# A routed expert stage on one core: blank rows in front of each expert's region instead of behind its last row, and last tiles that overlap

## The reference

```
x = x + ln(attn(ln(x)))                      # state-space block
logits = xf @ Wr + br; probs = softmax(logits)
vals, idx = top_k(probs, 2); w = vals / vals.sum(-1)
for ei in range(16):
    h = silu(xf @ W1[ei]) * (xf @ W3[ei])    # 128 -> 512
    y = layernorm(h @ W2[ei]) * gamma[ei] + beta[ei]
    out = out + combine[:, ei:ei + 1] * y
x = x + ln(out)
```

## Time and profile before

| What | Value |
|---|---|
| Median of 3 runs | 968.94 us (967.91 to 969.12) |
| Profiled execution | 968.34 us, of which the span of instructions is 966.5 us |
| Mean granted TensorE clock | 0.99 |
| PE busy | 933.1 us (97%) |
| DVE, ACT, POOL busy | 724.8, 688.3, 621.8 us |
| POOL stores of stage 2 (L698) | 143, 148.2 us busy |
| DMA share of the 16 engines | q1 18.4%, q0 5.2% |

### The profile page before, as it was taken

How to read it: one execution, slowest core, us unless ns; L and a number is a source line. 1 busy time by engine, 2 the same in 40 slices (tenths; PEclk the granted TensorE clock), 3 DMA queues, 4 the chain that set the end, 5 groups by cost and what they waited for, 6 DMA issues and landing times.

```text
span 966.5 us, 26600 instructions
## 1 busy us (share of the span) xinstructions
PE 933.1 (97%) x7177; PEld 826.0 (85%) x7177; DVE 724.8 (75%) x2524; ACT 688.3 (71%) x1355; POOL 621.8 (64%) x814
## 2 busy tenths in 40 slices
PE   7999999999999999998959999999999999999995
PEld 4777877888878877887949999999999999999962
DVE  2379999999999998898823777677677677777747
ACT  3777787777788787775215778777777777877626
POOL 2445677777777777775661666666666666576647
PEclk9999999999999999999979999999999999999998
DMA  4001322121111111101786211111111111121076
GB/s 137 12 12 34 93 95 84 58 73 54 56 57 50 56 40 42 40 23 42 263 311 192 69 50 49 46 52 51 44 50 50 45 50 47 45 53 49 19 274 248
DMA packets 52255, 75.25 MB, mean 78 GB/s; under 512 B 11103, under 2 KB 30689, under 8 KB 51472
## 3 DMA queue, kind: packets, MB, share of 16 engines
q1 hardware_dynamic: 41632, 54.61, 18.4%
q0 software_dynamic: 8672, 16.93, 5.2%
q10 hardware_dynamic: 1808, 2.02, 0.7%
HBM read 47.09 MB, written 27.41 MB: 77 GB/s over the span
## 4 chain that ended last, share of the span: by engine, by line
PE 79%; DVE 8%; POOL 6%; issue 5%; DMA 1%; ACT 1%; POOLq 0%; DVEq 0%; SPq 0%; ACTq 0%
PE pA L2106 11%; PE pR L2106 11%; PE pA L1665 11%; PE pB L2114 6%; PE pY L2114 5%; PE pY L1779 4%; PE pB L1691 3%; PE pB L1825 3%; PE pA L1680 3%; PE pY L1815 3%; POOL chosen_scratch L698 2%; PE pY L1798 2%; PE pY L1747 2%; PE pA L1636 2%; PE pR L1763 2%
## 5 line engine op out<-in xcount | busy, mean ns | idle before, releaser
L698 POOL DMA_INDIRECT chosen_scratch<-yo,got_id x143 | 148.2, 1036 | 93.7 <-issue 87.9
L1026 ACT ACTIVATE stage<-w_sb 128x1024 f32 x143 | 151.3, 1058 | 56.6 <-issue 56.5
L1545 DVE TENSOR_TENSOR hidT<-pR,sil 128x512 f32<-128x512 f32 x143 | 98.9, 692 | 80.1 <-ACT sil L1021 59.2
L612 POOL DMA_INDIRECT slots_scratch<-xrow,send_at x128 | 134.6, 1052 | 34.1 <-issue 31.2
L2106 PE MATMUL pA<-xsT,stage 128*128 128x128 f32 x1144 | 151.3, 275 | 0.4 <-ACT xsT L1010 0.4
L2106 PE MATMUL pR<-xsT,stage 128*128 128x128 f32 x1144 | 151.1, 275 | 0.0
L2106 PEld LDWEIGHTS pA<-xsT,stage 128*128 128x128 f32 x1144 | 139.2, 192 | 0.7 <-ACT xsT L1010 0.6
L2106 PEld LDWEIGHTS pR<-xsT,stage 128*128 128x128 f32 x1144 | 139.0, 192 | 0.0
L1665 PE MATMUL pA<-xn,taps 128*128 128x512 f32 x256 | 129.8, 593 | 1.0 <-ACT xn L763 1.0
L688 POOL TENSOR_TENSOR ers<-eve,neg_half 128x1 f32<-128x1 f32 x143 | 81.5, 570 | 57.3 <-DVE eve L1557 32.2
L1021 ACT ACTIVATE sil<-pA 128x512 f32<-128x512 f32 x143 | 85.3, 596 | 25.3 <-PE pA L2106 15.3
(11 more groups left out here) (233 smaller groups left out, 2099.1 us busy)
## 6 DMA issues: line engine op xcount, KB each, us to landing
got<-slots_scratch SPq DMA_DIRECT2D x143, 65.0 KB, 1.8
w_sb<-chosen_scratch SPq DMA_DIRECT2D x16, 512.0 KB, 5.4
w_sb<-in_w_dram SPq DMA_DIRECT2D x1, 6144.0 KB
xin<-in_x_dram SPq DMA_DIRECT2D x16, 256.0 KB
xr<-in_x_dram SPq DMA_DIRECT2D x16, 256.0 KB
x_scratch<-x SPq DMA_DIRECT2D x16, 256.0 KB
w_sb<-in_w_dram SPq DMA_DIRECT2D x4, 1024.0 KB, 8.2
fx<-x_scratch SPq DMA_DIRECT2D x1, 4096.0 KB
```

Of the source, the lines that this page charges most:

```text
L612: eng.indirect_dma_start(slots_d, bass.IndirectOffsetOnAxis(ap=send_at[:, s % 2, k, t:t + 1], axis=0), xrow[:, s % 2, k, t, :], None).then ...
L698: eng.indirect_dma_start(chosen_d, bass.IndirectOffsetOnAxis(ap=got_id[:, j % NGOT:j % NGOT + 1], axis=0), yo[:, q, :], None, bounds_check ...
L1026: eng.activation(stage[:, j % NSTAGE, :, :].rearrange("p k f -> p (k f)"), w13_sb[:, bass.ds(e, 1), :, :].rearrange("p o k f -> p (o k f)" ...
L1545: eng.tensor_tensor(hidT[:, p, :], pR[:, p, :], sil[:, p, :], ALU.mult).then_inc(hid_ready, 1)
```

## The change

Each region begins with 128 blank rows, and its own rows start behind them: `running` gets 128 added at the start of the kernel. These 16 blocks of blank rows do not depend on the routing and are written by one DMA in stage 1. An expert's last tile no longer starts at a multiple of 128 rows: it ends at the expert's last row, and so takes rows of its tile before once more (or blank rows from in front, where the expert has fewer than 128). Those rows are computed twice and written twice, with the same values, to the same rows of chosen_scratch. The table's chain gets the instructions for the new first rows. `store_tail`, `tail_at` and the semaphores around them go. `store(j)` also waits until the store of tile j - 1 has landed. NSLOT, the matmuls and all sizes of a tile stay.

```diff
--- before.py
+++ after.py
@@ -135,7 +135,9 @@
         shift = sb("shift", [P, NE])
         shift_step = sb("shift_step", [P, NE])
         ones_e = sb("ones_e", [P, NE])
-        tail_at = sb("tail_at", [P, NE], i32)
+        end_step = sb("end_step", [P, NE])
+        past_end = sb("past_end", [P, 2, NE])
+        slot_end = sb("slot_end", [P, 2])
         past = sb("past", [P, 2, NE])
         past_step = sb("past_step", [P, 2, NE])
         slot_cols = sb("slot_cols", [P, 4])
@@ -321,10 +323,6 @@
         ov = out.rearrange("s (p t) d -> s p t d", t=NT4)
         sum_bank = lambda g: w13_sb[:, 0, 0, :] if g == 0 else (pA, pB, pR, pY)[g % 8 // 2][:, g % 2, :]
 
-        def store_tail(eng, e):
-            row = eng.value_load(tail_at[0:1, e:e + 1], min_val=0, max_val=BLANK - P)
-            eng.dma_start(slots_d[bass.ds(row, P), :].rearrange("(p r) d -> p (r d)", r=8), blank[:, :]).then_inc(tails_stored, 16)
-
 
         blank_ready, blank_stored, e_loaded = sem("blank_ready"), sem("blank_stored"), sem("e_loaded")
 
@@ -337,7 +335,7 @@
         stage1_pe, stage1_act, stage1_pool = sem("stage1_pe"), sem("stage1_act"), sem("stage1_pool")
         stage1_dve = sem("stage1_dve")
         stage1_sp = sem("stage1_sp")
-        tables, tail_ready, tails_stored = sem("tables"), sem("tail_ready"), sem("tails_stored")
+        tables = sem("tables")
         cols_ready, cols_mm, table_ready = sem("cols_ready"), sem("cols_mm"), sem("table_ready")
         got_loaded = [sem(f"got_loaded{q}") for q in range(NGOT)]
         xs_t = sem("xs_t")
@@ -425,6 +423,8 @@
             load_x(3)
             load_x(4)
             load_x(5)
+            eng.dma_start(slots_d[0:BLANK, :].rearrange("(e r) d -> e r d", e=NE)[:, 0:P, :].rearrange("e (p r) d -> p e (r d)", r=8),
+                          blank[:, :].rearrange("p (o f) -> p o f", o=1).broadcast_to([P // 8, NE, 8 * ROW])).then_inc(blank_stored, 16)
             load_xr(1)
             store_x1(0)
             load_x(6)
@@ -473,16 +473,12 @@
             load_late()
             store_x1(15)
 
-            eng.wait_ge(tail_ready, 1)
-            for e in range(0, NE, 2):
-                store_tail(eng, e)
             eng.wait_ge(x1_stored, 16 * NS)
             eng.nop().then_inc(stage1_sp, 1)
             for q in (stage1_pe, stage1_act, stage1_pool, stage1_dve):
                 eng.wait_ge(q, 1)
 
-            eng.wait_ge(tails_stored, 16 * NE)
-            eng.wait_ge(blank_stored, 16)
+            eng.wait_ge(blank_stored, 32)
             for p in range(2):
                 eng.wait_ge(sent[p], NS // 2 * 2 * NT4 * 16)
             eng.wait_ge(table_ready, 1)
@@ -694,6 +690,8 @@
 
                 eng.wait_ge(yo_ready, j + 1)
                 eng.wait_ge(id_ready, j + 1)
+                if j:
+                    eng.wait_ge(stored[(j - 1) % 4], ((j - 1) // 4 + 1) * 16)
                 eng.sem_inc(pool_passed, 1)
                 eng.indirect_dma_start(chosen_d, bass.IndirectOffsetOnAxis(ap=got_id[:, j % NGOT:j % NGOT + 1], axis=0), yo[:, q, :], None,
                                        bounds_check=2 * NTOKENS - 1, oob_is_err=False).then_inc(stored[q], 16)
@@ -996,9 +994,6 @@
             eng.wait_ge(xft_ready, NS + 1)
             eng.nop().then_inc(stage1_act, 1)
 
-            eng.wait_ge(tail_ready, 1)
-            for e in range(1, NE, 2):
-                store_tail(eng, e)
             for q in (stage1_pe, stage1_dve, stage1_pool, stage1_sp):
                 eng.wait_ge(q, 1)
             eng.wait_ge(gb_loaded, 32)
@@ -1064,6 +1059,7 @@
                 eng.tensor_scalar(ndtw[:, :], dtw[:, :], -0.5, None, ALU.mult).then_inc(dve_consts, 1)
                 eng.tensor_scalar(ndtb[:, :], dtb[:, :], -0.5, None, ALU.mult).then_inc(dve_consts, 1)
                 eng.wait_ge(e_loaded, 16 * 6)
+                eng.tensor_scalar(running[:, :], running[:, :], float(P), None, ALU.add).then_inc(lower_ready, 1)
                 eng.tensor_copy(lower_b[:, :], lower_f[:, :]).then_inc(lower_ready, 1)
                 eng.memset(ones_b[:, :], 1.0).then_inc(lower_ready, 1)
                 eng.memset(chosen_b[:, 0:1, :], 0.0).then_inc(lower_ready, 1)
@@ -1337,9 +1333,6 @@
                                   running[:, :].rearrange("p (o e) -> p o e", o=1).broadcast_to([P, NT4, NE]), ALU.add).then_inc(pos_step, 1)
                 need(eng, pos_step, s, 3, 1)
                 eng.tensor_tensor(running[:, :], running[:, :], pB[:, 0, TOTAL:TOTAL + NE], ALU.add).then_inc(rank_read, 1)
-                if s == NS - 1:
-                    eng.wait_ge(rank_read, NS)
-                    eng.tensor_scalar(tail_at[:, :], running[:, :], slot_no[:, 0:1], None, ALU.add).then_inc(tail_ready, 1)
                 eng.tensor_tensor(placed[:, :, :, :], chosen[:, s % 2, :, :, :],
                                   place[:, :, :].rearrange("p (o t) e -> p o t e", o=1).broadcast_to([P, 2, NT4, NE]), ALU.mult).then_inc(pos_step, 1)
                 need(eng, pos_step, s, 3, 2)
@@ -1516,7 +1509,10 @@
             r.link(eng.tensor_tensor(count_i[:, :], running[:, :], region_sb[:, :], ALU.subtract))
             r.link(eng.memset(ones_e[:, :], 1.0))
             r.step(eng.memset(shift_step[:, NE - 1:NE], float(NOWHERE)))
-            r.step(eng.tensor_scalar(count_i[:, :], count_i[:, :], P - 1, None, ALU.add))
+            r.link(eng.memset(end_step[:, NE - 1:NE], float(BLANK + P)))
+            r.step(eng.tensor_tensor(end_step[:, 0:NE - 1], running[:, 1:NE], running[:, 0:NE - 1], ALU.subtract))
+            r.link(eng.tensor_tensor(end_step[:, NE - 1:NE], end_step[:, NE - 1:NE], running[:, NE - 1:NE], ALU.subtract))
+            r.step(eng.tensor_scalar(count_i[:, :], count_i[:, :], -1, None, ALU.add))
             r.step(eng.tensor_scalar(ntiles_i[:, :], count_i[:, :], P.bit_length() - 1, None, ALU.arith_shift_right))
             r.step(eng.tensor_copy(ntiles[:, :], ntiles_i[:, :]))
             r.step(eng.tensor_tensor_scan(tiles_to[:, :], ones_e[:, :], ntiles[:, :], 0.0, ALU.mult, ALU.add))
@@ -1527,11 +1523,15 @@
             r.step(eng.tensor_tensor(past[:, :, :], slot_no[:, :].rearrange("p (c o) -> p c o", o=1).broadcast_to([P, 2, NE]),
                                      tiles_to[:, :].rearrange("p (o e) -> p o e", o=1).broadcast_to([P, 2, NE]), ALU.is_ge))
             r.step(eng.tensor_tensor(past_step[:, :, :], past[:, :, :], shift_step[:, :].rearrange("p (o e) -> p o e", o=1).broadcast_to([P, 2, NE]), ALU.mult))
+            r.link(eng.tensor_tensor(past_end[:, :, :], past[:, :, :], end_step[:, :].rearrange("p (o e) -> p o e", o=1).broadcast_to([P, 2, NE]), ALU.mult))
             r.link(eng.tensor_reduce(slot_cols[:, 0:2], past[:, :, :], AX.X, ALU.add))
             r.step(eng.tensor_reduce(slot_cols[:, 2:4], past_step[:, :, :], AX.X, ALU.add))
+            r.link(eng.tensor_reduce(slot_end[:, :], past_end[:, :, :], AX.X, ALU.add))
             r.step(eng.scalar_tensor_tensor(out=slot_cols[:, 2:4], in0=slot_no[:, :], scalar=float(P), in1=slot_cols[:, 2:4], op0=ALU.mult, op1=ALU.add))
             eng.tensor_scalar(slot_cols[:, 0:2], slot_cols[:, 0:2], float(NE - 1), None, ALU.min).then_inc(cols_ready, 1)
-            eng.tensor_scalar(slot_cols[:, 2:4], slot_cols[:, 2:4], float(BLANK), None, ALU.min).then_inc(cols_ready, 1)
+            r.step(eng.tensor_scalar(slot_end[:, :], slot_end[:, :], running[:, 0:1], None, ALU.add))
+            r.step(eng.scalar_tensor_tensor(out=slot_cols[:, 2:4], in0=slot_cols[:, 2:4], scalar=float(2 * P), in1=slot_end[:, :], op0=ALU.add, op1=ALU.min))
+            eng.tensor_scalar(slot_cols[:, 2:4], slot_cols[:, 2:4], float(-P), None, ALU.add).then_inc(cols_ready, 1)
             eng.wait_ge(cols_mm, 1)
             eng.tensor_copy(slot_table[:, :], pA[0:1, 0, :]).then_inc(table_ready, 1)
             for q in (stage1_pe, stage1_act, stage1_pool, stage1_sp):
```

## The result

The changed kernel takes 1080.1 us, the median of four runs (1072.91 to 1087.63); the kernel before took 969.03 beside it (967.91 to 969.25). The ratio is 1.115, with a 95% interval of 1.107 to 1.123: slower, as forecast, but outside the range of 1013 to 1042. The profiled execution is the longest of the four, 1087.63 us with a span of 1085.5, against 966.5 before: 119.0 us more, of which 7.5 belong to this execution and not to the median. Lines of the file have moved up by two or four: the store is L696.

A forecast was written before the change was run, and what follows sets the result against it. The prediction took PE to bound the kernel, busy 97% of the span, with POOL setting the loop's pace after the change. It summed 968.3 + 67 - 5 + 2.5 = 1032.8, said 1032 us, range 1013 to 1042.

The forecast's parts named there:

- The step of the loop: Stage 2 store loop: with the new wait, stores start 3.23 us apart, where before it was 2.78.
- The first step: Start of the store loop, under the load of fx1: 6.5 us, from a longest landing of 5.6 plus 0.9.
- +67: Store loop: the new wait stretches it from 394.2 to 461.4 us; bounds about +39 and +83.
- More rows written: Stage 2 stores: each last tile writes up to 127 rows twice, at most 16 tiles of 143; taken as 0.
- the early blank store: Stage 1: one 1 MB DMA on SP and one added DVE instruction; cost 0 (0 to 0.3).
- Between the stages: Between stages 1 and 2: blank stores removed, table matmuls may get faster, DVE chain longer; -5 us taken.
- the bound of 507.5: Between the stages: earliest first transpose of stage 2 if the stall goes away, 8.5 us earlier.
- The end: After the last store: PE idles after keep_warm and the clock may fall in the pair sums; +2.5 us (0 to 5).
- A hidden wait: Store loop rival: release time is spent during the wait, step stays 2.79; 960 to 969 us, chance 0.08.
- a shorter step: Store loop rival: shorter landings or release, steps of 2.9 to 3.1 us; 985 to 1014 us, chance 0.12.
- a fallen clock in the loop: Store loop rival: PE's gaps drop the clock to 1.2 GHz; +400 us if it lasts, chance 0.05.
- The rival of no gain between the stages: Step stretches, but sends, gamma and beta stall PE, first transpose stays at 516; 1037 to 1039 us, chance 0.25.

The follow-up runs named there:

- m1_masked: The changed kernel without its wait; rows a last tile takes again get NOWHERE added to their number and are written once; 966.99 us, ratio 0.9965.
- e5_more_pe: The changed kernel with 20 nops added in PE's loop, which left no instruction in the trace; 1080.47 us, ratio 1.115.
- e4: The changed kernel with PE's W1 matmuls of tile j also waiting for the landing of store j - 6; 1068.98 us, ratio 1.103.
- e3: The changed kernel with half of the 512 hidden numbers left out of PE's stage 2 matmuls; 1059.12 us, ratio 1.096.
- e6: The changed kernel with six unused one-column matmuls added on PE in each tile; 1087.5 us, ratio 1.123.
- e7: The changed kernel with three quarters of the hidden numbers left out of PE's stage 2 matmuls; 1048.31 us, ratio 1.085.
- e2: The kernel before with only a wait in store j for the landing of store j - 2; 967.96 us, ratio 1.0005.
- e1: The kernel before with only the new wait, store j for the landing of store j - 1; 1082.61 us, ratio 1.120.

## Why the prediction was right and where it failed

**The step of the loop was right.** "So store j starts 2.3 + 0.93 = 3.23 us after store j - 1": the median is 3.25. The first step, 6.5 by forecast, is 6.44; the second, 3.7 by forecast, 3.25. ers and erw stand directly behind each store, as said. PE's busy share over the loop is 0.85, forecast 0.86, but that agreement is luck: the forecast was for steps of 3.23, while the loop's steps average 3.63, and in the normal step at 565.94 PE is busy for 3.06 of 3.25 us. From landing to start it is 0.94 us in nearly every step (3.62 in the one behind the 113th store). The 50 ns for the dispatch that the Trainium skill gives (page "DMA: Bandwidth & Descriptors", section "Anatomy of one DMA — SWDGE (gpsimd) path"), by which the wait would have been free, does not hold here.

**The step that failed** is the sentence "The median is the value that repeats, so I stay at +67", with the product behind it, 140 x 3.23. With a landing that nobody waits for, the median is all one needs. In a chain of waits each landing counts, and the sum goes by the mean. The missing 53.5 us (514.9 - 461.4) are in this execution: 46.7 of excess at stores that share their time with an instruction packet, 2.7 of the one step at 930, 2.8 from 3.25 instead of 3.23 over 140 steps, and about 1.3 of small ones (five steps have 1.24 us from landing to start and not 0.94). Without the excess at the packets this execution would have taken 1087.6 - 46.7 = 1040.9 us: the 1032.8 of the sum, with 2.1 more because the gain between the stages was smaller, 2.7 + 2.8 + 1.3 from the loop, 1.2 less at the end, and 0.4 of rounding and of time outside the spans. So the packets are the large miss and not the only one; that the line through four medians meets 1029.4 at no packet, near the forecast, proves nothing, since the price of a packet isn't constant.

Could it have been seen? The mean of the landings before hardly shows it (2.38 from the third store on; 26 of 32 packets came when the data was through), but the page shows q8 with 63 packets, and the two packets that came earlier in the step, 1.46 and 1.57 us behind a store, stood at landings of 2.98 and 3.83. What the trace of before could not show is where the packets would fall once PE waits for the store. It was wrong to have no term for it and to give no range for the mean of a landing.

**More rows written, the early blank store: 0.** Right; m1_masked's loop is 394.2 us, as before.

**Between the stages: -5.** In the profiled pair the first transpose moved from 515.98 to 513.03 and the first store from 526.96 to 524.02, so -2.9. The table's matmuls behaved as hoped:

```profile
495.97 1.03 PE L2086 MATMUL pA<-ident,slot_cols 128*1 128x128 f32 x8
497.16 0.27 PE L1636 MATMUL pA<-ident 128*128 128x128 f32 x1 [0.16 <-issue]
...
503.59 9.60 PE L1636 MATMUL pA<-ident 128*128 128x128 f32 x64 [0.22 <-issue]
505.13 0.68 DVE L1536 CAST slot_table<-pA 1x512 int32<-1x512 f32 x1 [9.33 <-remote]
...
506.89 6.99 SPq L489 DMA_DIRECT2D got<-slots_scratch  x7
...
513.03 0.27 PE L2098 MATMUL pB<-ident,got 128*128 128x128 f32 x1
```

The eight records take 1.03 us where they took 9, but the stall only begins right behind them, the cast comes at 505.13 as before, and keep_warm ends at 513. So the stall comes without the blank stores too. Nor do gamma and beta alone explain it: among the experiments that leave this stretch as it is in the changed kernel, the cast is at 505.47 in e5_more_pe, and at 496.95, 497.62, 497.25 and 495.24 in e4, e3, e6 and e7, with first transposes at 508.02, 508.44, 507.82 and 506.23; e3_half_pe for one:

```profile
497.52 9.20 PE L1636 MATMUL pA<-ident 128*128 128x128 f32 x80
508.44 0.30 PE L2098 MATMUL pB<-ident,got 128*128 128x128 f32 x1 [1.73 <-DMA got<-slots_scratch]
```

The stall comes in some executions and not in others. Both profiled ones of the main pair had it. Without it the first transpose is at 512.16 and 513.83 with the blank stores (e2, e1) and at 506.2 to 508.4 without them: 3.7 to 7.6 us. There the transpose waits for SP's load of the tile (1.73 us in the line above). So -5 and the bound of 507.5 were of the right size for executions without the stall, and this is luck in part, since I counted on the stall going away and it did not. What decides whether it comes is open.

**The end: +2.5.** From the last store's start to the end of the span it was 966.5 - 921.2 = 45.3 and is 1085.5 - 1038.88 = 46.6, so +1.3. PE starts its keep_warm at 1025.51, 13.4 us ahead of the last store (forecast 11.7), and the clock is at 0.72 on average from 1038 to 1050.

**Sum** of the profiled pair: -2.9 + 120.6 + 1.3 = 119.0, the difference of the spans.

**The rivals.** A hidden wait, a shorter step and a fallen clock in the loop (0.99) did not come. The rival of no gain between the stages was half right about the reason (not the blank stores) and wrong about the size. None of the rivals ended above 1042 but the clock's: all had the landing as one number.

## What to carry to other kernels

When a change puts a transfer's landing into the chain that sets the pace, ask for the mean and the tail of the landings, not the median, and ask which other packets can now fall on it: each 16384-byte instruction packet of PE cost 0.7 to 1.4 us here, by its place in the step, one for every 256 or so of PE's instructions, though PE's own loop had no gap before. A wait for the landing of the transfer just before costs the landing and another 0.94 us; the same wait two tiles back was free. Where an order of writes is only needed because rows are written twice, drop the second write (here with a number added to the row's address) and the wait goes with it.

## What the runs showed of the hardware

- In the changed kernel a store of 128 rows lands 2.31 us after its start, within 0.02 in 95% of the stores in whose time no instruction packet of 16384 bytes moves. In the kernels with the wait it lands later if one does: 2.4 to 3.7 us if the packet starts 0.4 to 1.2 us behind the store, and 3.3 to 4.3 if it starts 1.2 to 1.8 us behind. From 1.8 to 2.4 us it is either 3.8 to 4.5 or the usual 2.1 to 2.3, and from 2.6 us on the usual. The packets took 0.88 to 1.70 us themselves.
- The delay is that of one data packet of 16. In the changed kernel it ended 0.39 to 0.48 us behind the instruction packet's end in all 31 cases from 1.2 us on, with the other 15 through by 2.02 us.
- The place of these packets in the step is nearly the same through an execution (mostly 1.26 to 1.6 us in the changed kernel) and another in another (half of them at 0.7 to 1.0 in e5_more_pe, the same program as it turned out; its span is 10 us shorter).
- Between the stages DVE can stand still for 9 to 10 us (from 495 or 496 to 505) in one execution and not in the next of the same stretch of program. PE is then busy for 1.65 (before) and 3.92 us (after) of the 6 from 497 to 503, and for all 6 in e2_wait_two_back.
